# TensorE's completion signals moved from matmuls to drains, in one half of a transformer-and-experts kernel

## What is computed

```
x = x + tanh(g_xattn[0]) * L0_xattn(layernorm(x), ctx)     # 16 heads of 64, q and k normalised, no softmax,
                                                           # then layernorm and an MLP 128 -> 512 -> 128 with gelu
x = x + tanh(g_ffn[0])   * L0_ffn(layernorm(x))            # 64 experts of width 88, 8 chosen per token,
                                                           # plus one shared expert of width 176
x = x + tanh(g_xattn[1]) * L1_xattn(layernorm(x), ctx)     # one head of 32, sigmoid of the scores
x = x + tanh(g_ffn[1])   * L1_ffn(x)                       # rms norm, 16 experts of width 128, 4 per token
```

## Time and profile before

| what | us |
|---|---|
| median of the runs | 1425.95 |
| lowest and highest run | 1423.86, 1428.04 |
| the profiled execution, first to last instruction | 1921.7 |

### The profile page before, as it was taken

How to read it: one execution, slowest core, us unless ns; L and a number is a source line. 1 busy time by engine, 2 the same in 40 slices (tenths; PEclk the granted TensorE clock), 3 DMA queues, 4 the chain that set the end, 5 groups by cost and what they waited for, 6 DMA issues and landing times.

```text
span 1921.7 us, 22687 instructions
## 1 busy us (share of the span) xinstructions
PE 1227.9 (64%) x6314; PEld 831.3 (43%) x6333; DVE 873.9 (45%) x2519; ACT 580.6 (30%) x993; POOL 500.0 (26%) x528
## 2 busy tenths in 40 slices
PE   3999872200599884810059936566774766685998
PEld 2666541100366652710058836566653322234443
DVE  4888658100377655400012203223343844577665
ACT  2666421100266531400025513333431211122332
POOL 0000000777200000277700063443242245600000
PEclk9999985655699996855569967787885877796999
DMA  9992000222000110522236534444530011100000
GB/s 285 327 330 106 1 0 7 78 78 78 23 0 0 38 23 33 167 90 91 92 111 189 177 122 128 140 144 123 154 99 22 18 36 40 46 21 4 1 11 11
DMA packets 102672, 165.23 MB, mean 86 GB/s; under 512 B 12676, under 2 KB 66444, under 8 KB 101492
## 3 DMA queue, kind: packets, MB, share of 16 engines
q1 hardware_dynamic: 82022, 122.77, 20.2%
q0 software_dynamic: 20608, 41.98, 7.3%
HBM read 74.52 MB, written 90.18 MB: 86 GB/s over the span
## 4 chain that ended last, share of the span: by engine, by line
PE 45%; another core or an unknown queue 23%; DVE 11%; issue 10%; DMA 5%; ACT 4%; SPq 1%; DVEq 1%; ACTq 0%
PE PS L589 4%; PE PS L600 4%; PE PS L1552 4%; DMA sb_A<-sorted_rows 4%; PE PS L1413 3%; PE PS L1449 3%; PE PS L1439 3%; PE PS L1432 3%; PE PS L1418 3%; PE PS L1570 2%; PE PS L1545 2%; PE PS L1506 2%; DVE sb_A L467 2%; PE PS L1424 2%
## 5 line engine op out<-in xcount | busy, mean ns | idle before, releaser
L746 POOL DMA_INDIRECT sb_Y<-sorted_out,sb_POS x256 | 246.0, 961 | 474.4 <-DVE sb_X L1296 210.4
L1310 DVE SCALAR_TENSOR_TENSOR sb_A<-sb_A,PS 128x88 f32<-128x88 f32 x384 | 91.8, 300 | 500.8 <-ACT sb_A L872 276.4
L1552 PE MATMUL PS<-sb_WGU,sb_A 128*128 x768 | 164.6, 366 | 225.7 <-issue 116.2
L732 POOL DMA_INDIRECT sorted_rows<-sb_XR,sb_POS x256 | 246.5, 963 | 80.4 <-issue 80.4
L1552 PEld LDWEIGHTS PS<-sb_WGU,sb_A 128*128 128x128 f32 x768 | 140.3, 225 | 235.3 <-issue 233.7
L600 PE MATMUL PS<-sb_A,sb_RT 128*128 128x512 f32 x256 | 143.7, 647 | 57.5 <-DVE sb_A L467 41.7
L321 ACT ACTIVATE sb_A<-sb_A 128x512 f32<-128x512 f32 x128 | 80.6, 630 | 254.3 <-DVE sb_A L467 169.9
L867 ACT ACTIVATE sb_A<-PS 128x512 f32<-128x512 f32 x96 | 57.3, 597 | 306.7 <-remote 159.1
L459 DVE TENSOR_SCALAR sb_A<-PS,sb_VEC 128x512 f32<-128x512 f32 x128 | 95.7, 748 | 97.9 <-PE PS L589 67.5
L714 POOL COPY sb_XR<-sb_ZT 128x512 f32 x8 | 4.9, 615 | 501.9 <-DVE sb_ZT L1134 501.9
L589 PE MATMUL PS<-sb_WGU,sb_RT 128*128 (+1 forms) x256 | 134.1, 611 | 1.6 <-DVE sb_A L459 1.5
(11 more groups left out here) (249 smaller groups left out, 2032.8 us busy)
## 6 DMA issues: line engine op xcount, KB each, us to landing
sorted_rows<-sb_RT SPq DMA_DIRECT2D x2, 18432.0 KB, 88.8
sb_A<-sorted_rows SPq DMA_DIRECT2D x96, 384.0 KB
sorted_out<-sb_A SPq DMA_DIRECT2D x96, 256.0 KB
sb_WGU<-in_wgu SPq DMA_DIRECT2D x1, 5632.0 KB, 77.2
sorted_rows<-sb_XR,sb_POS POOLq DMA_INDIRECT x256
sb_Y<-sorted_out,sb_POS POOLq DMA_INDIRECT x256
sb_RW<-in_wd SPq DMA_DIRECT2D x1, 2816.0 KB
sb_X<-in_x SPq DMA_DIRECT2D x2, 1024.0 KB
```

Source lines behind the costliest of these rows:

```text
L732: pool.indirect_dma_start(out=xs[c], in_=XR[:, t, :], in_offset=None, out_offset=bass.IndirectOffsetOnAxis(ap=POS[:, b * TOPK + k:b * TOPK ...
L746: pool.indirect_dma_start(out=GBUF[r][:, k * D:(k + 1) * D], out_offset=None, in_=ys[c], in_offset=bass.IndirectOffsetOnAxis(ap=POS[:, b * ...
L1310: ins = v.scalar_tensor_tensor(EH[:, t, :], ESI[:, t, :], XB[r][:, t, one(e[t] + D)], gu_bank[r % 2][:, t, EI:2 * EI], ALU.mult, ALU.mult)
L1552: ins = mm(gu_bank[r % 2][:, t, 0:2 * EI], EXT[:, t * P:(t + 1) * P], WGU[:, e[t], :], start=True, stop=True)
```

## The change

A helper `after(drained, ins)` is added in the `pe` block. Where `drained` is true it issues a drain on TensorE and gives it back, and the signal is put on this drain; else the signal stays on the matmul. `drained` is true in attention, MLP and routing of chunk 1 (`d = c > 0`) and in the experts of chunk 0 (`DRAIN_EXPERTS = (True, False)`). The last matmuls of routing (`t_rank`) and all of layer 2 stay as they were. No wait, no matmul and no other engine's program changes. The diff, with repeats cut:

```diff
+DRAIN_EXPERTS = (True, False)
...
             mm = nc.tensor.matmul
+
+            def after(drained, ins):
+                return nc.tensor.drain() if drained else ins
+
...
             def attention(c):
                 lo, hi = chunk_tiles(c)
+                d = c > 0
 
                 def T(b):
                     pe.wait_ge(a_z, b + 1)
                     nc.tensor.transpose(PS[:, 0, 0:P], ZT[:, 0:D], ID)
-                    nc.tensor.transpose(PS[:, 0, P:P + NC_CTX], ZC, ID[0:NC_CTX, 0:NC_CTX]).then_inc(a_t, 1)
+                    ins = nc.tensor.transpose(PS[:, 0, P:P + NC_CTX], ZC, ID[0:NC_CTX, 0:NC_CTX])
+                    after(d, ins).then_inc(a_t, 1)
 
                 def q(b):
                     pe.wait_ge(a_qk, b + 1)
                     for j in range(2):
                         ins = mm(PS[:, 1 + j, :], QNT, WQ[:, 512 * j:512 * (j + 1)], start=True, stop=True)
-                    ins.then_inc(a_q, 1)
+                    after(d, ins).then_inc(a_q, 1)
...
                         if h % 8 == 7:
-                            ins.then_inc(a_g, 1)
+                            after(d, ins).then_inc(a_g, 1)
...
-            def transposes(ready, done, g):
+            def transposes(ready, done, g, d):
...
-                ins.then_inc(done, 1)
+                after(d, ins).then_inc(done, 1)
 
             def mlp(c):
                 lo, hi = c * GC, (c + 1) * GC
+                d = c > 0
 
                 def up(g):
                     pe.wait_ge(m_te, g + 1)
                     for n in range(4):
-                        mm(bank(1 + n), W1[:, n * P:(n + 1) * P], XT, start=True, stop=True).then_inc(m_h, 1)
+                        ins = mm(bank(1 + n), W1[:, n * P:(n + 1) * P], XT, start=True, stop=True)
+                        after(d, ins).then_inc(m_h, 1)
...
             def experts(c):
                 o = c * SS
+                d = DRAIN_EXPERTS[c]
                 pe.wait_ge(t_ter, 16 * (c + 1))
...
-                    ins.then_inc(e_t, 1)
+                    after(d, ins).then_inc(e_t, 1)
...
-                    ins.then_inc(e_gu, 1)
+                    after(d, ins).then_inc(e_gu, 1)
...
-                    ins.then_inc(e_ht, 1)
+                    after(d, ins).then_inc(e_ht, 1)
...
-                    ins.then_inc(e_y, 1)
+                    after(d, ins).then_inc(e_y, 1)
```

More of the change, by code:

```diff
@@ L1418, in k @@
                         ins = mm(PS[0:NC_CTX, 3 + j, :], KNT, WK[:, 512 * j:512 * (j + 1)], start=True, stop=True)
-                    ins.then_inc(a_k, 1)
+                    after(d, ins).then_inc(a_k, 1)
                 def qT(b):
@@ L1424, in qT @@
                         ins = nc.tensor.transpose(bank(5, 2)[:, j * P:(j + 1) * P], QN[:, j * P:(j + 1) * P], ID)
-                    ins.then_inc(a_qt, 1)
+                    after(d, ins).then_inc(a_qt, 1)
                 def p(b):
@@ L1432, in p @@
                         ins = mm(PS[:, 5 + j, :], VN, KN[0:NC_CTX, 512 * j:512 * (j + 1)], start=True, stop=True)
-                    ins.then_inc(a_p, 1)
+                    after(d, ins).then_inc(a_p, 1)
                 def g(b):
@@ L1450, in o @@
                                  start=(j == 0), stop=(j == 7))
-                    ins.then_inc(a_o, 1)
+                    after(d, ins).then_inc(a_o, 1)
                 T(lo)
@@ L1489, in down @@
                                      W2[:, n * D:(n + 1) * D], start=(n == 0), stop=(n == 3))
-                    ins.then_inc(m_o, 1)
-                transposes(m_z, m_t, lo)
+                    after(d, ins).then_inc(m_o, 1)
+                transposes(m_z, m_t, lo, d)
                 up(lo)
                 with pe.Fori(lo, hi - 1) as g:
-                    transposes(m_z, m_t, g + 1)
+                    transposes(m_z, m_t, g + 1, d)
                     down(g)
@@ L1507, in rest @@
                         if n % 2:
-                            ins.then_inc(r_gu, 1)
+                            after(d, ins).then_inc(r_gu, 1)
                     for t in range(G):
                         ins = mm(PS[:, 7, t * E:(t + 1) * E], XT[:, t * P:(t + 1) * P], GWT[:], start=True, stop=True)
-                    ins.then_inc(r_l, 1)
+                    after(d, ins).then_inc(r_l, 1)
                 def down(g):
@@ L1518, in down @@
                                      start=(n == 0), stop=(n == 1))
-                    ins.then_inc(r_o, 1)
-                transposes(r_z, r_t, lo)
+                    after(d, ins).then_inc(r_o, 1)
+                transposes(r_z, r_t, lo, d)
                 rest(lo)
                 with pe.Fori(lo, hi - 1) as g:
-                    transposes(r_z, r_t, g + 1)
+                    transposes(r_z, r_t, g + 1, d)
                     down(g)
```

## The result

The changed kernel takes 1681.91 us, the median of 2 runs (1679.89 to 1683.92), against 1425.95 us: a ratio of 1.18, with a 95% interval from 1.174 to 1.185. It is 256 us slower; 217 were forecast.

What follows compares the result with a forecast made beforehand. TensorE was taken as the bound in calm stretches, its late signals as the profiled execution's alone. Attention 54, MLP 9, routing 5 and chunk 0's experts 149 make 217 us; 1426 + 217 = 1643 us, range 1457 to 1745.

Steps and rivals of the forecast that it cites:

- the late time: Beside GpSimd's DMAs in the profiled execution, TensorE's completion signals come late: 558 us, nearly all absent from the timed runs.
- The 36 us: Rest of the timed runs' 62 us after scatter(1)'s 26, left for late signals and whatever lies around the span.
- A drain holds the sequencer: On TensorE, a drain holds back the sequencer until the array is idle; if later matmuls passed, cost near 0.
- The price of a drain: On TensorE: 0.16 us matmul tail, 0.10 first weight load, 0.10 drain and decoding; 0.36 us, between 0.16 and 0.57.
- The loop's end: In chunk 1's attention, the branch and address work that ran beneath `o` become bare: 0.5 us an iteration.
- the dear end: Upper end of the range: clock stays low in chunk 0's experts and drains cost 0.57 us each, 1745 us.
- I take the middle, 7.1 us: Experts of chunk 0: a slot between 5.7 us at full clock and 8.5 at low; the stage 149 us more.
- The cover: Experts of chunk 0: chunk 1's loads wait for scatter(1), holding the stage to about 201 us instead of 175, 26 us.
- Clock low: Rival for chunk 0's experts: slots of 8.5 us, 214 us more, 1708 us in all; over 1708 had chance 0.17.
- Clock high: Rival for chunk 0's experts: slots of 5.7 us, 81 us more, 1575 us; with cheap drains (1457 to 1575) chance 0.18.
- Nothing: Rival for all drains: they hold nothing back or their hold falls beneath the waits, 1426 us; chance 0.08.
- faster: Rival beside the scatters: matmul signals are late in timed runs too, a drain's is not; 37 us gained, 1389; chance 0.12.

Runs made afterwards that it cites:

- second profile: The kernel before, unchanged, profiled once more: a profiled span of 1426.4 us, and 1428.21 us in its timed runs (ratio 1.000).
- table edit: The changed kernel with the expert table read ahead of the drain for `down` and for three `gu` of four, drains kept: 1567.53 us (ratio 1.098).

## Why the prediction was right, and where it was off

**What bounds the kernel.** Right. TensorE is the bound in the treated attention, and a hold on it shows one for one. That the late time belongs to the profiled execution alone was right too, but the 558 us were too many: the second profile is 1921.7 - 1426.4 = 495 us shorter. The 36 us which were left for late signals and the surroundings of the span were not late signals: no wait of that kind was found in the second profile. Some 21 of them are the experts of chunk 1, whose 47 slots average 183.9 / 47 = 3.91 us where calm ones were taken at 3.47. Some 11 are layer 2, where the half on chunk 1 was taken as the measure for the half on chunk 0: from the last slot to the end of its last stage, 997.6 to 1418.4, it takes 420.8 us in the second profile, where the prediction's subtraction leaves 410. Some 2 lie around the span (1428.2 - 1426.4).

**A drain holds the sequencer.** Right. The 364 drains last 1112 ns in the middle, about as long as the groups before them, and groups stopped overlapping. The Trainium skill (PSUM — Partial Sum Buffer, Engine vs sequencer instructions) says that a drain waits for the engine to go fully idle. The trace agrees: `p` starts 0.22 us after `q`'s modelled end, where it had started 0.16 before it.

**The price of a drain.** Near: 0.36 us forecast. An iteration grew by 2.87 us. The loop's gap is 0.58 against 0.22 for the next longest, so the bare branch is taken as 0.36, and 2.51 / 8 = 0.31 is left for a drain. The loop's end was put at 0.5. The stage grew by 44.6 us (16 x 2.87 is 46) where the step gave 54. MLP and routing came out lower in the same way, 7.4 for 9 and 3.8 for 5. The ends of the price do not follow from the terms: the low one, 0.16, leaves out the 0.10 of the first weight load, and the 1745 us at the dear end counts 0.21 us more only for the 172 drains outside the experts' stage; with all 364 it would be 1784.

**The experts of chunk 0.** The mechanism was right in both halves, and the size was off. The step that failed is "I take the middle, 7.1 us": the slot takes 8.16, and the stage costs 204.8 us more instead of 149. The end points themselves were low as well: the groups and gaps of one slot give 9.06 us at the lower clock (forecast 8.5, though its own terms of 6.8 and 1.8 add to 8.6), and the same 2.10 us of gaps with 1.46 + 0.65 + 0.61 + 1.15 us of groups at full clock give 5.97 (forecast 5.7). The measured slot lies 71% of the way to the slow end. That fits the clock: with 71% of the work at half clock, 0.71 x 9.06 / 8.16 = 79% of the time is spent there, a mean of 0.61 where the trace has 0.59. By this account, which is worked out and not measured by a run of its own, 5.97 - 3.91 = 2.06 of the 4.25 us are bare work and 2.19 the clock. So 97 us of the stage's 205 are drains, tails and table reads, about 103 are clock, and 5 the longer end. The evidence for the low side stood in the forecast: the stage starts after a long idle stretch, and every slot is idle in four pieces. The sum came nearer than this term by luck: attention, MLP and routing were 12 us too dear (68 for 55.8) while the experts were 56 too cheap.

**Scatter(1).** The held stage was right, 201.6 us for 201, and its cover is used up after the change (187 us to spare). The cover itself was not 26 us but about 5: without the hold the stage would take 183.9 + 12 = 196 us, since the slots average 3.91 us and not 3.47.

**The rivals.** Clock low had 1708, and the result lies between it and the forecast. Clock high had 1575, with the table reads bare and the clock full. The table edit's 1567.53 is near it, and its slot of 5.69 us too, but by another way: its reads are mostly hidden and its clock is 0.87. "Nothing" and "faster" are excluded by the timed runs, and the second also at its root: the second profile of the kernel before has no late signal. The sign that I named for it, that the stretch from 330 to 500 us fills, did appear (27.2 us of TensorE before, 143.9 after), but the kernel before fills it even better by itself, 160.3. A span that fell from 1921.7 to 1682.1 us stood beside timed runs that rose by 256.

## What to carry to other kernels

Put the signal on the last matmul of a group, and where a drain must stand on an engine's path, count not the drain but what it bares: the tail, the sequencer's reads and branches behind it, and then the clock of an array that idles between the groups. What the sequencer needs next, read before the drain. When a profiled execution is far longer than the timed runs, profile the same kernel again before explaining any wait in it.

## What the runs showed of the hardware that was not expected

- The granted clock was worth more here than the work that kept it up: 890 more matmul instructions in the experts' stage made it 68 us shorter from first to last slot, at clock 0.99 against 0.59, all drains kept.
- Four drains a slot at clock 0.59 and two a slot at 0.94: the clock does not fall by so much per drain.
- One profiled execution of a kernel can be 35% longer than its timed runs, with TensorE's signals 19 and 62 us late beside GpSimd's indirect DMAs. A second one of the same kernel had none, at 1426.4 us. Why the first had them is open.
- A drain on an array that is already idle costs 0.07 us in the timeline and 0.09 in the timed runs.
